# Down projections of the second pair of sequences as transposed seven-product quarters

## The chip, the cores and the metric

The kernel runs on one core of one Trainium2 chip. The metric is the device time of one execution in microseconds (us). The engines are TensorE (PE in the rows, its weight loads PEld), VectorE (DVE), ScalarE (ACT), GpSimd (POOL) and SyncE (SP, whose row SPq is the DMA queue that it issues on).

## The reference

For four sequences of 512 tokens with 512 features: a cross-attention weight is added to `x`, and then a routed feed-forward block. Cut to what the change touches:

```python
gate = einsum('btd,edf->ebtf', x, Wg); up = einsum('btd,edf->ebtf', x, Wu)   # 8 experts, D = F = 512
mid = silu(gate) * up
out = einsum('ebtf,efd->ebtd', mid, Wd)          # the down projection
y = x + einsum('bte,ebtd->btd', weights, out)    # router weights per token and expert
```

Two experts also have low-rank additions to Wg, Wu and Wd; the kernel merges these into the weights first. All is float32. The kernel splits each float32 operand into a high and a low part and makes three passes (high x high, low x high, high x low) for each product.

## The kernel before, in words

After attention and the first expert (up to about 205 us) come `STEPS` = 14 rounds of one expert each on a pair of sequences: rounds 0 to 6 on sequences 0 and 1, rounds 7 to 13 on sequences 2 and 3 (`SWAP` = 7 is the first of these). Two sequences and the halves of the 512 features give a 2 x 2 block problem, and so gate and up are computed by Strassen's method in Winograd's form: seven products where a plain one has eight. Each of gate and up is worked in two halves of output rows, so that a round k has four "quads": j = 4k (gate, first half), 4k+1 (gate, second half), 4k+2 (up, first half), 4k+3 (up, second half). `quad(j, pending)` (before L1630) issues products 1, 5, 6, 3, 2, 7, each of two feature tiles by three passes, six matmuls of 128x128 weights on 512 columns. Product 4 of quad j (`fourth`) is issued inside the next quad, after its product 5, since it waits for VectorE to have read the bank (`c_made[C22]`).

The sums around the products are VectorE's and ScalarE's. For each quad VectorE makes four sums of weight quarters (`piece_sums`, L1168), ScalarE rounds the seven weight operands to their high parts (`piece_high_part`, L818), VectorE subtracts for the low parts (`piece_low_part`, L1182), and only then may product 1 begin (`piece_ready`). Three piece buffers rotate; SyncE loads one when the quad that used it has finished its product 4 (`load_next_piece`, L372). From the products ScalarE copies P1, P5 and U2 out of PSUM (`copy_p1`, `copy_p5`, `copy_u2`, L828 to L844), VectorE combines (`combine`, L1206), ScalarE applies silu (`gate_silu`), VectorE multiplies gate by up (`make_mid`, L1219), and each of the eight mid tiles gets a high part (ScalarE) and a low part (`mid_low_part`, L1262).

The down projection of round k-1 is plain: `down_half` (L1673) for each sequence, 4 token tiles by 4 feature tiles by 3 passes, 96 matmuls for the two, in the middle of round k, on the four banks `tiles`. Its weights are one load of 1 MB with one high and one low part (`wd_high_part`, `wd_low_part`). VectorE adds the four results of each half into `xacc`, scaled by the token's router weight (`add_down`, L1235), since tokens are on the partitions.

Each engine runs a list written out by hand, in program order; a wait holds all that is behind it on the same engine. VectorE's list for a round is the loop at L1386.

Of the kernel before, what the change touches and what calls it, by code (L numbers as in the profile page):

```python
# [10 lines left out]
P = 128  # L11
# [46 lines left out]
GATE, UP = 0, 1  # L58
# [9 lines left out]
def xattn_ffn_kernel(nc, x, xT, ctxT, wkT, bk, gamma, beta, wg, wu, wd, loraT, lora, wr, temperature, out):  # L68
# [6 lines left out]
    with ExitStack() as ctx:  # L75
# [33 lines left out]

        lora_a, lora_b, lora_w = (at(name, kb, shape) for name, kb, shape in  # L110
# [31 lines left out]
        s1_sb = nc.alloc_sbuf_tensor_at("s1_sb", [P, S], fp32, offset=beta_at)  # L142
        x_spill = nc.dram_tensor("x_spill", [2, 2, P, KT * S], fp32, kind="Internal").ap()
        x21_spill = nc.dram_tensor("x21_spill", [P, 2 * S], fp32, kind="Internal").ap()
        acc_spill = nc.dram_tensor("acc_spill", [P, 2 * TT * D], fp32, kind="Internal").ap()
# [140 lines left out]
        piece_ready = [sem(f"piece_ready{i}") for i in range(3)]  # L286
        wd_loaded = sem("wd_loaded")
# [53 lines left out]

        def mids_before(j):
# [17 lines left out]
        def _(sp):  # L360
# [4 lines left out]
            def load_piece(j):  # L365
                k, m, f = j // 4, j % 4 // 2, j % 2
                source = weights_of(k, m).rearrange("(k p) f -> p k f", p=P)
                for g, cols in ((0, f + 2), (1, f)):
                    sp.dma_start(piece[j % 3][:, 2 * g:2 * g + 2, :].rearrange("p g (k c) -> p (g k) c", k=2),
                                 source[:, :, cols * P:(cols + 1) * P]).then_inc(piece_loaded[j % 3], 16)  # L370

            def load_next_piece(j):  # L372

                if j < 4 * STEPS:
                    sp.wait_ge(p_mm[4], j - 2)
                    load_piece(j)
# [109 lines left out]
            for k in range(1, STEPS):  # L486
# [23 lines left out]
                sp.wait_ge(d_mm, 8 * k)  # L510
                load_wd(k)
                if k == SWAP:
# [3 lines left out]
                    sp.dma_start(xacc[:, 2 * TT * D:], acc_spill).then_inc(acc_loaded, 16)  # L516
# [5 lines left out]
                if k < len(LORA_JOBS):  # L522
                    store_merged(k)
            for i in range(2 * TT):
                store_out(2 * TT + i, 8 * (STEPS - 1) + i + 1)
# [4 lines left out]
        def _(pool):  # L530
# [101 lines left out]
            pool.wait_ge(x_stored, 64)  # L632
            load_again(0, 0, 1)
            load_again(1, 2, 3)
            load_again(0, 2, 2)


        @block.scalar
        def _(act):
# [178 lines left out]
            def piece_high_part(j):  # L818
                if j < 4 * STEPS:
                    act.wait_ge(piece_summed[j % 3], 4 * (j // 3) + 4)  # L820
                    nc.scalar.activation(piece_hi[j % 3][:, :, :], piece[j % 3][:, 1:8, :], ACT.Copy)\  # L821
# [1018 lines left out]
```

## Time and profile before

| | |
|---|---|
| median of three runs | 1055.22 us (1054.95 to 1056.51) |
| the profiled execution | 1055.69 us, of which the span of the profile is 1054.0 us |
| PE busy | 1042.4 us, 99% |
| PE weight loads | 853.0 us, 81% |
| DVE busy | 708.8 us, 67% |
| ACT busy | 449.5 us, 43% |
| POOL busy | 50.4 us, 5% |

Busy time of an engine is time covered by at least one of its instructions. A single matmul of 512 columns is shown with 389 ns, yet matmuls overlap: what one costs in a stream is the distance of two starts. The same is to be seen on DVE, where an instruction can begin before the end of the one before it. The granted TensorE clock was full in every slice.

### The profile page before, as it was taken

To read this page: it belongs to the slowest core of one execution; us is meant where nothing else is said; L and a number is where in the kernel's file an instruction comes from. 1 tells how busy PE (TensorE), PEld (TensorE's weight loads), DVE (VectorE), ACT (ScalarE), POOL (GpSimd) and SP (SyncE) were. 2 spreads that over 40 slices of the span, in tenths; PEclk is the share of its full clock that TensorE was granted. 3 is DMA by queue.
4 is the path that set the end of the run, shared out by engine and by line. 5 is a ranking of instruction groups with operands and counts; after the bars stand their busy time and mean duration, and the time that the engine had idled before them with its cause. 6 is when DMAs were issued, how large, how long until landed. Compare 5 with 4: busy or idle time off the path is not lost.

```text
span 1054.0 us, 12230 instructions
## 1 busy us (share of the span) xinstructions
PE 1042.4 (99%) x4680; PEld 853.0 (81%) x4680; DVE 708.8 (67%) x1212; ACT 449.5 (43%) x653; POOL 50.4 (5%) x62
## 2 busy tenths in 40 slices
PE   8999999999999999999999999999999999999998
PEld 5887787878888888888888888788888888888887
DVE  7878678877484866838487684847566473838544
ACT  4654363554442543444344344525334343524430
POOL 2511121100000000000000000000000000000000
PEclk9999999999999999999999999999999999999999
DMA  9410104334151322415135537202021121112012
GB/s 297 156 50 1 81 21 160 106 94 140 60 148 32 125 75 81 140 61 145 35 115 165 177 103 239 59 23 80 23 78 41 60 60 60 41 40 79 21 41 80
DMA packets 91307, 94.73 MB, mean 90 GB/s; under 512 B 4464, under 2 KB 67056, under 8 KB 90352
## 3 DMA queue, kind: packets, MB, share of 16 engines
q1 hardware_dynamic: 90096, 90.73, 27.4%
q0 software_dynamic: 864, 3.15, 1.0%
q8 instruction: 37, 0.61, 0.2%
q14 instruction: 22, 0.18, 0.1%
q10 hardware_dynamic: 288, 0.07, 0.0%
HBM read 76.63 MB, written 17.30 MB: 89 GB/s over the span
## 4 chain that ended last, share of the span: by engine, by line
PE 86%; DVE 8%; issue 2%; ACT 2%; DMA 1%; POOL 0%; SPq 0%; DVEq 0%
PE gate_up L1621 15%; PE gate_up L1623 15%; PE gate_up L1622 15%; PE tiles L1508 10%; PE tiles L1510 10%; PE tiles L1509 10%; PE gate_up L1579 2%; PE gate_up L1580 2%; PE gate_up L1585 2%; PE tiles L1544 1%; DVE piece_lo L1187 1%; DMA wd_raw<-in_wd_dram 1%; DVE mids_lo L1265 1%; DVE xacc L1239 1%; DVE tx_lo L1248 0%
## 5 line engine op out<-in xcount | busy, mean ns | idle before, releaser
L1621 PE MATMUL gate_up<-xT_hi,piece_hi 128*128 128x512 f32 x448 | 174.8, 390 | 1.0 <-DVE mids L1226 0.6
L1508 PE MATMUL tiles<-wd_hi,mids_hi 128*128 128x512 f32 x448 | 174.4, 389 | 0.4 <-DVE mids_lo L1265 0.4
L1623 PE MATMUL gate_up<-xT_lo,piece_hi 128*128 128x512 f32 x448 | 174.4, 389 | 0.0
L1622 PE MATMUL gate_up<-xT_hi,piece_lo 128*128 128x512 f32 x448 | 174.4, 389 | 0.0
L1509 PE MATMUL tiles<-wd_lo,mids_hi 128*128 128x512 f32 x448 | 174.3, 389 | 0.0
L1510 PE MATMUL tiles<-wd_hi,mids_lo 128*128 128x512 f32 x448 | 174.3, 389 | 0.0
L1239 DVE SCALAR_TENSOR_TENSOR xacc<-tiles,rw,xacc 128x512 f32<-128x512 f32 x112 | 78.0, 750 | 138.5 <-PE tiles L1510 138.5
L1187 DVE TENSOR_TENSOR piece_lo<-piece,piece_hi 128x1024 fp32r<-128x1024 f32 x112 | 118.2, 1097 | 28.9 <-ACT piece_hi L821 27.6
L1621 PE MATMUL gate_up<-tx_hi,piece_hi 128*128 128x512 f32 x336 | 130.9, 389 | 0.3 <-DVE gates L1216 0.3
L1622 PE MATMUL gate_up<-tx_hi,piece_lo 128*128 128x512 f32 x336 | 130.8, 389 | 0.0
L1623 PE MATMUL gate_up<-tx_lo,piece_hi 128*128 128x512 f32 x336 | 130.8, 389 | 0.0
L834 ACT ACTIVATE gate_up<-gate_up 128x512 f32<-128x512 f32 x56 | 32.6, 582 | 208.7 <-PE gate_up L1623 201.2
L861 ACT ACTIVATE mids_hi<-mids 128x512 fp32r<-128x512 f32 x112 | 70.4, 629 | 85.5 <-DVE mids L1226 45.4
L821 ACT ACTIVATE piece_hi<-piece 128x1792 fp32r<-128x1792 f32 x56 | 95.2, 1700 | 24.0 <-DVE piece L1180 24.0
L1621 PEld LDWEIGHTS gate_up<-xT_hi,piece_hi 128*128 128x128 f32 x448 | 84.1, 188 | 20.9 <-issue 1.4
L1508 PEld LDWEIGHTS tiles<-wd_hi,mids_hi 128*128 128x128 f32 x448 | 84.1, 188 | 18.3 <-DVE mids_lo L1265 0.8
L1623 PEld LDWEIGHTS gate_up<-xT_lo,piece_hi 128*128 128x128 f32 x448 | 84.1, 188 | 17.5
L1510 PEld LDWEIGHTS tiles<-wd_hi,mids_lo 128*128 128x128 f32 x448 | 84.1, 188 | 17.4
L1509 PEld LDWEIGHTS tiles<-wd_lo,mids_hi 128*128 128x128 f32 x448 | 84.1, 188 | 17.4
L1622 PEld LDWEIGHTS gate_up<-xT_hi,piece_lo 128*128 128x128 f32 x448 | 84.1, 188 | 17.1
L1265 DVE TENSOR_TENSOR mids_lo<-mids,mids_hi 128x512 fp32r<-128x512 f32 x112 | 77.0, 688 | 6.9 <-ACT mids_hi L861 4.9
L1621 PEld LDWEIGHTS gate_up<-tx_hi,piece_hi 128*128 128x128 f32 x336 | 63.1, 188 | 13.9 <-DVE gates L1216 0.7
(176 smaller groups left out, 1406.2 us busy)
## 6 DMA issues: line engine op xcount, KB each, us to landing
piece<-in_wg_dram SPq DMA_DIRECT2D x40, 256.0 KB, 3.2
piece<-in_wu_dram SPq DMA_DIRECT2D x40, 256.0 KB, 3.3
wd_raw<-in_wd_dram SPq DMA_DIRECT2D x10, 1024.0 KB, 5.3
piece<-merged SPq DMA_DIRECT2D x32, 256.0 KB, 3.3
merged<-lora_w SPq DMA_DIRECT2D x6, 1024.0 KB, 4.3
x_back<-x_spill SPq DMA_DIRECT2D x9, 512.0 KB, 5.3
wd_raw<-merged SPq DMA_DIRECT2D x4, 1024.0 KB, 5.6
out_dram<-xacc SPq DMA_DIRECT2D x16, 256.0 KB, 4.1
```

Source lines behind the costliest of these rows:

```text
L821: nc.scalar.activation(piece_hi[j % 3][:, :, :], piece[j % 3][:, 1:8, :], ACT.Copy)\
L834: nc.scalar.activation(gate_up[:, BANK_C, :], gate_bank(j), ACT.Copy).then_inc(s1_made, 1)
L861: nc.scalar.activation(mids_hi[h][:, f, :], mids[h][:, f, :], ACT.Copy).then_inc(mids_hi_made, 1)
L1187: ins = nc.vector.tensor_tensor(piece_lo[j % 3][:, first:last, :], piece[j % 3][:, first:last, :], plain(piece_hi[j % 3][:, first - 1:last ...
L1239: nc.vector.scalar_tensor_tensor(tile_of(b, t), tiles[:, t, :], rw[:, (b * TT + t) * E + s:(b * TT + t) * E + s + 1], tile_of(b, t), ALU.m ...
L1265: nc.vector.tensor_tensor(mids_lo[h][:, f, :], mids[h][:, f, :], plain(mids_hi[h][:, f, :]), ALU.subtract)\
L1508: nc.tensor.matmul(dst, w_h, x_h, start=first, stop=False)
L1509: nc.tensor.matmul(dst, w_h, x_l, start=False, stop=False)
L1510: return nc.tensor.matmul(dst, w_l, x_h, start=False, stop=last)
L1621: nc.tensor.matmul(dst, w_h, x_h, start=first and kt == 0, stop=False, skip_group_check=True)
L1622: nc.tensor.matmul(dst, w_l, x_h, start=False, stop=False, skip_group_check=True)
L1623: ins = nc.tensor.matmul(dst, w_h, x_l, start=False, stop=last and kt == 1, skip_group_check=True)
```

## The change

For rounds 7 to 12 (the second pair, all but the last expert) the down projection is no longer plain. It is computed transposed (output features on the partitions, tokens along the free dimension) and by the same seven products, in two halves `down_quad(d)`, d = 2(k-7) and 2(k-7)+1. The last round's down projection (13) stays plain.

- Down weights are now quarters like gate's and up's: they are loaded as pieces, and get `piece_sums`, a high and a low part each. `QUADS` lists the order of all pieces; in rounds 8 and on it is gate 0, gate 1, down 0, down 1, up 0, up 1.
- The mid tiles need operand sums of their own: `mix_of` makes T1 to T4 for both feature tiles, and seven operands for each of the two have a high and a low part.
- With tokens along the free dimension the router weight can no longer be a scalar per partition. Gates are multiplied by a router row instead (`scale_gates`, two instructions of 1024 elements for each half), the rows being made by one transpose, a store and broadcast loads (`turn_rw`, `load_rw_rows`).
- The results are added into a transposed accumulator `acc_t` (`add_u2_and_p5`, `add_c12`, `add_c11`, `add_c22`, `add_c21`), with three copies by ScalarE for each half.
- In the last round `acc_t` is turned back by 32 TensorE transposes in two groups (`turn_back`) and added to `xacc` (`add_turned_back`), which is reloaded only in round 13 (before: round 7).

PE's order in rounds 8 to 13, and VectorE's list for such a round:

```diff
+            for k in range(SWAP + 1, STEPS):
+                j, d = 4 * k, 2 * (k - SWAP - 1)
+                quad(j, True)
+                quad(j + 1, True)
+                down_quad(d)
+                down_quad(d + 1)
+                quad(j + 2, False, d + 1)
+                if k == STEPS - 1:
+                    turn_back(0)
+                quad(j + 3, True)
             down_half(STEPS - 1, 0, 4 * STEPS - 1)
```

```diff
+            def operands_of_first(k):
+                combine(k, UP, 0, C12)
+                make_mid(k, 0, C12)
+                if k > SWAP:
+                    piece_low_part(NUMBER[k, UP, 1])
+                piece_low_part(NUMBER[k + 1, GATE, 0])
+                combine(k, UP, 0, C22)
+                make_mid(k, 0, C11)
+                make_mid(k, 0, C22)
+                mix_of(k, 0, T1)
+                operand_low_part(k, 0, B11)
+                mix_of(k, 0, T2)
+                mix_of(k, 0, T3)
+                operand_low_part(k, 0, T1)
+                operand_low_part(k, 0, B22)
+                make_mid(k, 0, C21)
+                mix_of(k, 0, T4)
+                combine(k, UP, 1, C12)
+                make_mid(k, 1, C12)
+                operand_low_part(k, 0, T2)
+                operand_low_part(k, 0, T3)
+                operand_low_part(k, 0, B21)
+                operand_low_part(k, 0, T4)
...
+            for k in range(SWAP + 1, STEPS):
+                j, d = 4 * k, 2 * (k - SWAP - 1)
+                last = k == STEPS - 1
+                combine(k - 1, UP, 1, C22)
+                make_mid(k - 1, 1, C11)
+                piece_sums(NUMBER[k, GATE, 1])
+                mix_of(k - 1, 1, T1)
+                operand_low_part(k - 1, 1, B11)
+                make_mid(k - 1, 1, C22)
+                piece_low_part(NUMBER[k, GATE, 1])
+                mix_of(k - 1, 1, T2)
+                mix_of(k - 1, 1, T3)
+                operand_low_part(k - 1, 1, T1)
+                operand_low_part(k - 1, 1, B22)
+                make_mid(k - 1, 1, C21)
+                mix_of(k - 1, 1, T4)
+                combine(k, GATE, 0, C12)
+                operand_low_part(k - 1, 1, T2)
+                operand_low_part(k - 1, 1, T3)
+                combine(k, GATE, 0, C22)
+                operand_low_part(k - 1, 1, B21)
+                operand_low_part(k - 1, 1, T4)
+                piece_sums(NUMBER[k - 1, DOWN, 0])
+                combine(k, GATE, 1, C12)
+                piece_low_part(NUMBER[k - 1, DOWN, 0])
+                combine(k, GATE, 1, C22)
+                if not last:
+                    scale_gates(k, 0)
+                piece_sums(NUMBER[k - 1, DOWN, 1])
+                add_u2_and_p5(d)
+                add_c12(d)
+                piece_low_part(NUMBER[k - 1, DOWN, 1])
+                add_c11(d)
+                add_c22(d)
+                piece_sums(NUMBER[k, UP, 0])
+                if not last:
+                    scale_gates(k, 1)
+                add_c21(d)
+                add_u2_and_p5(d + 1)
+                piece_low_part(NUMBER[k, UP, 0])
+                add_c12(d + 1)
+                add_c11(d + 1)
+                add_c22(d + 1)
+                piece_sums(NUMBER[k, UP, 1])
+                add_c21(d + 1)
+                if last:
+                    combine(k, UP, 0, C12)
+                    piece_low_part(NUMBER[k, UP, 1])
+                    make_mid(k, 0, C12)
+                    combine(k, UP, 0, C22)
+                    make_mid(k, 0, C11)
+                    mid_low_part(k, 0, C12)
+                    add_turned_back(0)
+                    make_mid(k, 0, C22)
...
+                    mid_low_part(k, 0, C21)
+                    wd_low_part(k)
+                    combine(k, UP, 1, C22)
+                    add_turned_back(1)
...
+                else:
+                    piece_sums(NUMBER[k + 1, GATE, 0])
+                    operands_of_first(k)
```

The load of a piece, ScalarE's order around a down quad, and what `down_quad` waits for:

```diff
+            def load_next_piece(n):
+                if n >= len(QUADS):
+                    return
+                k, which, m = QUADS[n - 3]
+                if which == DOWN:
+                    sp.wait_ge(q_mm, q_done(4, 2 * (k - SWAP) + m))
+                else:
+                    sp.wait_ge(p_mm[4], 4 * k + 2 * which + m + 1)
+                load_piece(n)
...
+                copy_q_u2(d)
+                piece_high_part(NUMBER[k - 1, DOWN, 1])
+                copy_q1(d + 1)
+                copy_q5(d + 1)
+                copy_q_u2(d + 1)
+                piece_high_part(NUMBER[k, UP, 0])
...
+            def down_quad(d):
+                n = NUMBER[SWAP + d // 2, DOWN, d % 2]
+                pe.wait_ge(piece_ready[n % 3], (n // 3 + 1))
...
+                down_product(d, 1, down_bank(d), first=True)
...
+                down_product(d, 5, tiles[:, BANK_B, :], first=True)
+                if d % 2 == 0:
+                    fourth(4 * (SWAP + 1 + d // 2) + 1)
+                else:
+                    down_fourth(d - 1)
...
+                down_product(d, 6, down_bank(d))
...
+                down_product(d, 3, tiles[:, BANK_B, :], last=True)
+                down_product(d, 2, tiles[:, BANK_C, :], last=True)
...
+                down_product(d, 7, down_bank(d))
```

## Rows read from the trace of the kernel before

**Rows 1.** The page's head and its section 1: share of the span.

```profile
span 1054.0 us, 12230 instructions
...
PE 1042.4 (99%) x4680; PEld 853.0 (81%) x4680; DVE 708.8 (67%) x1212; ACT 449.5 (43%) x653; POOL 50.4 (5%) x62
```

**Rows 2.** Windows: us, PE, PEld, DVE, ACT, POOL busy (x), PEclk, DMA share, GB/s.

```profile
757.90:817.80 59.90, 59.90 (x266) 49.58 (x265) 36.95 (x59) 24.30 (x33) 0.00 (x0) 1.00 0.18 53
```

**Rows 3.** PE's waits after 640 us: total, times, longest; two rows in all.

```profile
PE gate_up L1621 <- DVE mids L1226: 0.3, 1, 0.3
```

**Rows 4.** Timeline of PE: start, us, engine, line; first matmuls of four stretches.

```profile
648.25 0.39 PE L1621 MATMUL gate_up<-xT_hi,piece_hi 128*128 128x512 f32 x1
...
869.67 0.39 PE L1621 MATMUL gate_up<-xT_hi,piece_hi 128*128 128x512 f32 x1
...
871.03 0.39 PE L1621 MATMUL gate_up<-tx_hi,piece_hi 128*128 128x512 f32 x1
...
1027.43 0.39 PE L1508 MATMUL tiles<-wd_hi,mids_hi 128*128 128x512 f32 x1
```

**Rows 5.** Timeline of DVE in round 11: starts that follow one another without a wait.

```profile
888.24 2.79 DVE L1239 SCALAR_TENSOR_TENSOR xacc<-tiles,rw,xacc 128x512 f32<-128x512 f32 x4 [9.37 <-PE tiles L1510]
...
899.11 0.68 DVE L1229 TENSOR_TENSOR mids<-gates,gate_up 128x512 f32<-128x512 f32 x1
...
899.71 0.69 DVE L1265 TENSOR_TENSOR mids_lo<-mids,mids_hi 128x512 fp32r<-128x512 f32 x1
...
901.51 2.08 DVE L1187 TENSOR_TENSOR piece_lo<-piece,piece_hi 128x1024 fp32r<-128x1024 f32 x2
...
903.52 0.69 DVE L1265 TENSOR_TENSOR mids_lo<-mids,mids_hi 128x512 fp32r<-128x512 f32 x1
...
904.12 2.36 DVE L1195 TENSOR_TENSOR wd_lo<-wd_raw,wd_hi 128x1024 fp32r<-128x1024 f32 x2
...
906.39 0.68 DVE L1226 TENSOR_TENSOR mids<-gates,gate_up 128x512 f32<-128x512 f32 x1
...
913.72 0.42 DVE L1175 TENSOR_TENSOR piece<-piece 128x256 f32<-128x256 f32 x1
...
915.19 0.68 DVE L1212 TENSOR_TENSOR gates<-u_sb,gate_up 128x512 f32<-128x512 f32 x1
```

**Rows 6.** Timeline of DVE: an instruction that reads what the one before it wrote.

```profile
895.78 0.69 DVE L1212 TENSOR_TENSOR mids<-u_sb,gate_up 128x512 f32<-128x512 f32 x1 [3.30 <-PE gate_up L1623]
...
896.58 0.69 DVE L1233 TENSOR_TENSOR mids<-gates,mids 128x512 f32<-128x512 f32 x1
```

**Rows 7.** Timeline: from PE's products to ScalarE and VectorE.

```profile
873.75 0.39 PE L1621 MATMUL gate_up<-xT_hi,piece_hi 128*128 128x512 f32 x1
...
873.95 0.60 ACT L844 ACTIVATE u_sb<-gate_up 128x512 f32<-128x512 f32 x1 [0.76 <-PE gate_up L1623]
...
874.45 1.70 ACT L821 ACTIVATE piece_hi<-piece 128x1792 fp32r<-128x1792 f32 x1
...
875.38 0.69 DVE L1212 TENSOR_TENSOR gates<-u_sb,gate_up 128x512 f32<-128x512 f32 x1 [3.30 <-PE gate_up L1623]
...
876.18 2.09 DVE L1187 TENSOR_TENSOR piece_lo<-piece,piece_hi 128x1024 fp32r<-128x1024 f32 x2
```

**Rows 8.** From a finished product 4 to a load, and the loads' landing times.

```profile
631.93 0.39 PE L1508 MATMUL tiles<-wd_hi,mids_hi 128*128 128x512 f32 x1
...
632.12 0.92 SPq L369 DMA_DIRECT2D piece<-in_wu_dram  x2
...
DMA to landing us min/median/max: 2.8/3.2/5.9
...
xacc<-acc_spill SPq DMA_DIRECT2D x1, 2048.0 KB, 11.5
```

**Rows 9.** Timeline of PE: sixteen transposes and the matmul after them.

```profile
115.38 1.91 PE L1526 MATMUL gate_up<-w_raw 128*128 128x128 f32 x16
...
117.04 0.48 PE L1508 MATMUL tiles<-w_hi,mid_hi 128*128 128x512 f32 x1
```

More of the change, by code:

```diff
@@ L57 @@
 SWAP = POSITIONS - 1
-GATE, UP = 0, 1
+GATE, UP, DOWN = 0, 1, 2
+QUADS = [(k, which, m) for k in range(SWAP + 1) for which in (GATE, UP) for m in range(2)] \
+    + [(k - (which == DOWN), which, m) for k in range(SWAP + 1, STEPS) for which in (GATE, DOWN, UP) for m in range(2)]
+NUMBER = {quad: n for n, quad in enumerate(QUADS)}
+B11, T1, B22, T2, T3, B21, T4 = range(7)
+OPERAND = {1: B11, 5: T1, 6: T2, 3: B22, 2: B21, 7: T3, 4: T4}
 BANK_B, BANK_C = 1, 2
@@ L485, in _ @@
             store_merged(0)
-            for k in range(1, STEPS):
+            for k in range(1, SWAP + 1):
                 if k < len(LORA_JOBS):
@@ new lines, in operand_low_part, with add_to_turned @@
+            def operand_low_part(k, kt, o):
+                dve.wait_ge(operand_hi_made, 14 * (k - SWAP) + 7 * kt + o + 1)
+                raw, hi, lo = operand_of(o, kt)
+                nc.vector.tensor_tensor(lo, raw, plain(hi), ALU.subtract).then_inc(operand_ready, 1)
+            def add_to_turned(d, c, source):
+                m = d % 2
+                h, tile = 1 if c in (C12, C22) else 0, m if c in (C12, C11) else m + 2
+                to = acc_t[:, tile, h, :]
+                nc.vector.tensor_tensor(to, to, source, ALU.add).then_inc(q_added, 1)
@@ new lines, in add_c21, with add_turned_back @@
+            def add_c21(d):
+                dve.wait_ge(q_mm, q_done(4, d))
+                if d >= 2:
+                    dve.wait_ge(q_added, q_add("c21", d - 2))
+                add_to_turned(d, C21, down_bank(d))
+            def add_turned_back(h):
+                dve.wait_ge(acc_loaded, 16)
+                for t in range(TT):
+                    dve.wait_ge(back_mm, 4 * h + t + 1)
+                    nc.vector.tensor_tensor(tile_of(2 + h, t), tile_of(2 + h, t), tiles[:, t, :], ALU.add).then_inc(back_added, 1)
@@ L1417, in _ @@
                     combine(k, GATE, 1, C22)
-                    combine(k, UP, 0, C12)
+                    scale_gates(k, 0)
+                    scale_gates(k, 1)
+                    piece_sums(j + 4)
+                    operands_of_first(k)
+                    break
                 elif k > 0:
@@ L1628, in fourth, with down_product @@
                 product(j, 4, gate_bank(j), last=True)
-            def quad(j, pending):
+            def down_product(d, i, dst, first=False, last=False):
+                n = NUMBER[SWAP + d // 2, DOWN, d % 2]
+                hi, lo = piece_hi[n % 3], piece_lo[n % 3]
+                pe.wait_ge(operand_ready, 14 * (d // 2) + 7 + OPERAND[i] + 1)
+                for kt in range(2):
+                    cols = slice(kt * P, (kt + 1) * P)
+                    w_h, w_l = hi[:, COMBO[i] - 1, cols], lo[:, COMBO[i], cols]
+                    raw, x_h, x_l = operand_of(OPERAND[i], kt)
+                    nc.tensor.matmul(dst, w_h, x_h, start=first and kt == 0, stop=False, skip_group_check=True)
+                    nc.tensor.matmul(dst, w_l, x_h, start=False, stop=False, skip_group_check=True)
+                    ins = nc.tensor.matmul(dst, w_h, x_l, start=False, stop=last and kt == 1, skip_group_check=True)
+                ins.then_inc(q_mm, 1)
@@ L1779, in _ @@
             pe.wait_ge(mid_made, EARLIER + B * FT + UNIT_CREDIT)
-            for k in range(STEPS):
+            for k in range(SWAP + 1):
                 j = 4 * k
```

356 lines of the change are left out of this document (301 added, 55 removed).

## The prediction

> **What bounds the kernel now.** I read the page's section 1 first: PE is busy 99% of the span, DVE 67%, ACT 43% [rows 1]. Then the windows by round: a round of the second pair takes 59.9 us, PE covers all of it, DVE 36.95 us, ACT 24.3 us, and the granted clock is 1.00, the 2.4 GHz level [rows 2]. The waits confirm it: after 640 us PE waited for another engine twice, 0.5 us in all [rows 3]. So TensorE is the bound, and removed matmuls are removed time as long as the others keep up. What one costs is read from starts, not durations: two products of six matmuls start 1.36 us apart [rows 4], 226.7 ns for a matmul. A round has 4 quads of 42 matmuls and 96 for the down projection, 264 x 0.2267 = 59.85 us.
>
> The question is then whether DVE, with 23 us to spare in a round, keeps up with what the change gives it.
>
> **PE's gain.** A down projection goes from 96 matmuls to 2 x 42 = 84, in rounds 8 to 13: 72 x 0.2267 = 16.3 us less. PE's minimum for a round is 42 products x 1.36 = 57.1 us.
>
> **PE's addition.** 32 transposes: sixteen took 1.66 us before the next matmul started [rows 9], so 3.3 us, and one more in round 6 with its wait, some 0.2 us beside ScalarE's conversions. If all else hid, the sum would be 1055.2 - 16.3 + 3.5 = 1042.4 us.
>
> **DVE's load in a round.** Distances of starts [rows 5]: an instruction on 512 elements 0.60 us (899.11 to 899.71); the two of a piece's low part 2.01; two on 1024 elements 2.27; the four of `piece_sums` 1.47; one that reads what the instruction ahead of it wrote takes 0.20 more [rows 6]. The load before: 24 x 0.60 + 4 x 1.47 + 4 x 2.01 + 2.27 + 8 `add_down` (four cover 2.79) 5.4 + 0.4 = 36.4 us, against 36.95 measured [rows 2], so the count holds. After, in rounds 8 to 12: on 512 elements 8 `combine`, 8 `make_mid`, 8 `mix_of`, 14 `operand_low_part` and 12 adds, 50 x 0.60 = 30.0; `scale_gates` 4 x 1.14 = 4.5; six sums 8.8; six low parts 12.0; six close dependences 1.2. That is 56.6 us, against PE's 57.1. Mixes, scalings and adds are new, but have the form of instructions shown (both operands in SBUF, or one in PSUM). The nearest slower row, `add_down` at 0.68, would give 58.2; nothing in a row speaks for less than 0.60. I take 0.60.
> Here a rule can be weighed. In the trace an instruction lasts 0.69 us and the next starts after 0.60 [rows 5]. By the Trainium skill, "VectorE: DVE Perf Modes", section "The DRAIN you can't avoid", the next instruction does not start until the pipeline is empty. By that rule the 50 would cost 0.69 each, 4.5 us more a round; the trace disagrees for this kernel, so I don't count it.
>
> ACT gains 6 copies (0.50 us apart [rows 7]), 6 more operand roundings, two piece roundings of 1.7 for one of 1.9: about 8 us on 24.3. It is not a bound, but it stands in a chain below. At nothing I cost POOL's identity and its zeroing of `acc_t` (POOL is idle after the first fifth, and the first add comes in round 8), the router rows' loads (asked for half a round ahead; in round 7 they take the place of the 2 MB reload in SP's queue, behind the stores of the first pair and ahead of a piece that is held by its buffer anyway), and the 1 MB weight load of rounds 7 to 12, which goes. If the rows came late in round 7, `scale_gates` would hold S once, by a microsecond or two.
>
> **Whether DVE at 99% can keep pace.** Only without idling, and its list has waits on PE in it. I follow one round. Number PE's products: gate quads 0 to 6 and 7 to 13, down quads 14 to 20 and 21 to 27, up quads 28 to 34 and 35 to 41; the third place of each quad is the product 4 of the quad before. S is when DVE starts `combine(k, UP, 0, C12)`. It needs place 32 done, plus 0.27 us (product 3 starts at 873.75 and so ends at 875.11, DVE starts at 875.38 [rows 7]). F is when PE starts place 9 of the next round, product 4 of gate 0, which waits for `combine(k+1, GATE, 0, C22)`.
>
> S to F on DVE is one unbroken run: 34 instructions on 512 elements (19 in `operands_of_first`, 15 at the head of the next round) 20.4 us, three low parts 6.0, one `piece_sums` 1.47, four close dependences 0.8: 28.7 us. PE has 18 products there (33 to 41, 0 to 8), 24.5 us, and ends up waiting. From F, PE must do places 9 to 32, 24 x 1.36 = 32.6, and 0.27, before the next S. So a round can't be shorter than 28.7 + 32.6 + 0.3 = 61.6 us, though both engines have less than 57.2 us of work. That is already over 59.85.
>
> Three further waits lie on this loop.
> (a) The piece rounded for the next quad stands behind the copy of U2 in ScalarE's list (`copy_u2`, `copy_q_u2`). End of product 6 to copy 0.20, copy 0.50, rounding 1.73 to DVE's start (873.75, 873.95, 874.45, 876.18 in [rows 7]), low part 2.10, 0.05 to PE: 4.58 us. PE has three products left in the quad, 4.08 us. So 0.5 us before each of places 14, 21 and 28: 1.5 us. Behind the waiting DVE are the accumulations; they have room (8 us of work in 10).
> (b) `piece_sums` of the next round's gate 0 stands ahead of `operands_of_first`. Its buffer is freed by place 30. From there: 0.19 us to the first of two issues, 0.46 to the second, landing 3.2 [rows 8], 0.05, sums 1.47: S at 5.4 us after place 30, instead of 2.72 + 0.27 = 3.0. Costs 2.4 us. DVE idles, and all operands are queued behind it. Ends: 2.0 with the shortest landing of 2.8, 5.1 with the longest of 5.9; I take the median.
> (c) The low part of up 1 stands after S, so PE waits some 3.7 us at place 35. This is not on the loop: PE still reaches place 8 before DVE frees it.
> A round: 61.6 + 1.5 + 2.4 = 65.5 us. Bounds: 61.6 with neither, and 68 with 0.68 for the new forms in S to F, the slower landing in part, and 0.1 to 0.2 us for PE's restart after each of four waits, which no row shows cleanly.
>
> **The sum against the profiled execution.** Round 7's up 0 starts at 648.25 [rows 4]; nothing before it moves. Place 30 ends 4.08 later, at 652.33; S of round 7 by (b) at 657.7. The next round has no low part of up 1 in the run: S of round 8 at 657.7 + 63.5 = 721.2. Four rounds more: 721.2 + 4 x 65.5 = 983.2 for S of round 12. From there F, then places 9 to 30 with three waits of 0.5: 28.7 + 29.9 + 1.5 + 0.1 = 60.2, so place 30 of round 13 ends at 1043.4.
> The tail, in us from there. `acc_spill`, 2 MB, is asked for only now and took 11.5 to land [rows 8]; it is moved from round 7, where it delayed nobody, to round 13, where `add_turned_back(0)` stands ahead of `make_mid(k, 0, C22)` in DVE's list. So DVE waits until 12.1 and turns back until 14.5; `make_mid` C22 ends at 15.1. ScalarE rounds that mid ahead of `copy_p5`, and PE's place 39 waits for that copy until 16.3 (it would be there at 12.6). Then places 39 and 40, 16 transposes and 41: to 22.2. `combine` C22, then the first tile of `add_turned_back(1)`: the last `down_half` starts at 23.8, at 1067.2. In the kernel before it started at 1027.43 [rows 4] and the span ended 26.6 later. So 1067.2 + 26.6 = 1093.8, and 1.7 for what lies around the span (1055.69 - 1054.0): 1095.5 us. The profiled execution stands 0.5 us over the median. Forecast 1095 us, 3.8% slower.
>
> **The rivals.**
> 1. PE stays the bound and the gain comes. For it: DVE's sum of work is under PE's, and 23 us were free. Then only the tail costs: without its waits 1042.4, with the 5.5 us by which the reload holds the last `down_half` (23.8 against 15.0 + 3.3) 1047.9 us. It decides on the other side once a round is under 59.85 us. For that the loop S to F to S would have to be 1.8 us shorter than its instructions alone, and that needs starts under 0.55 us apart. 6%.
> 2. The loop is there, but (a) and (b) are smaller: rounds of 61.6 to 63.5 us. With neither, S of round 7 at 655.3, then 59.6 and 4 x 61.6, 58.7 to the end of place 30, 23.8 of tail and 28.3 to the end: 1072 us. With rounds of 63.5, about 1083. 17%.
> 3. PE's clock falls. It was 1.00 throughout [rows 2], but PE never stood still for 3.7 us there, as it would at place 35 and at the tail. By the Trainium skill, "TensorE: Matmul & The Clock Gate", section "HAM oscillation — how this bites in real kernels", idle gaps of this kind bring the array back to half clock. Its price from rows: a product at 1.2 GHz takes 2.7 us. A few are absorbed, since PE is ahead of DVE between S and F; were all of places 35 to 41 and the next 7 slow, PE would be late at place 8 by 6.5 us, and five rounds cost 33 us: 1127 us. 5%.
> 4. Within 0.2% of before: what DVE adds to a round and the 2.7 us that PE saves in it cancel. A coincidence, 2%.
> That the change doesn't do what it says would show as 1055 us and is in rival 4.
>
> **How the numbers follow.** The forecast, a round of 64 to 67 us and the end between 1085 and 1105, has 70%; it is the likeliest. The range goes down into rival 2 and up over slower restarts: 1073 to 1112 us. A change of under 0.2% can't be told from none in this measurement. Faster by more 6%, within 2%, slower 92%.
>
> **What would show each step.** Windows by round: about 65.5 us each from round 8 on, DVE busy 57, PE busy under 58. PE's waits: on DVE `gates` (`combine`) once or twice a round, on `piece_lo` four times, the one at up 1 the longest (3 to 4 us). DVE's waits: `piece` on the DMA some 2 to 3 us a round. Matmuls still 226.7 ns apart, clock 1.00. In the tail, a wait of some 4 us of `xacc` on the reload. I am wrong if DVE's starts are closer than 0.6 us, or if PE's waits on DVE total less than 3 us a round.

## The result, and the profile after

The changed kernel takes 1099.92 us, median of three runs (1099.79 to 1100.25), against 1055.22: a ratio of 1.0419 with a 95% interval of 1.0404 to 1.0435. The forecast was 1095 us, in a range of 1073 to 1112.

The page of the changed kernel, head and section 1, and the granted clock of section 2:

```profile
span 1098.2 us, 12671 instructions
...
PE 1050.6 (96%) x4641; PEld 844.5 (77%) x4641; DVE 832.0 (76%) x1412; ACT 497.9 (45%) x732; POOL 55.0 (5%) x65
...
PEclk9999999999999999999999999989999999998999
```

Against [rows 1], PE issues fewer matmuls and still takes longer; no engine is at its limit over the span. DVE does 123 us more.

Windows of the changed kernel (us, then PE, PEld, DVE, ACT and POOL busy, granted clock, DMA share, GB/s): one round from S to S, then two stretches of 4 us right after the longest wait of PE in that round.

```profile
922.24:988.69 66.45, 61.08 (x254) 47.90 (x252) 56.58 (x91) 32.48 (x46) 0.00 (x0) 0.97 0.19 56
926.00:930.00 4.00, 4.00 (x11) 3.12 (x11) 4.00 (x6) 0.96 (x2) 0.00 (x0) 0.57 0.02 4
930.00:934.00 4.00, 4.00 (x19) 3.28 (x18) 3.92 (x8) 3.51 (x8) 0.00 (x0) 1.00 0.19 58
```

Where [rows 2] had 59.90 us with PE busy in all of it, a round is 66.45 us; DVE is busy in 56.58 of them, and idle in the other 10.

PE's waits after 640 us (total, times, longest), which were two rows in [rows 3], 0.5 us together:

```profile
PE gate_up L1987 <- DVE piece_lo L1374: 18.5, 11, 3.5
PE gate_up L1987 <- ACT p_sb L931: 5.9, 7, 1.3
PE tiles L2005 <- DVE piece_lo L1374: 4.0, 12, 0.3
PE gate_up L1987 <- DVE mids L1403: 3.3, 3, 1.7
PE gate_up L1987 <- DVE mids L1415: 2.2, 6, 0.4
PE tiles L1873 <- DVE xacc L1540: 1.5, 1, 1.5
```

DVE's waits from 720 to 1045 us in the same kernel:

```profile
DVE acc_t L1499 <- ACT down_u L980: 10.3, 10, 2.0
DVE gates L1399 <- PE gate_up L1989: 9.5, 5, 1.9
DVE piece L1364 <- DMA piece<-in_wg_dram: 9.0, 3, 3.1
DVE acc_t L1499 <- PE tiles L2007: 6.8, 5, 1.8
DVE piece L1364 <- DMA piece<-merged: 5.9, 2, 3.0
```

The two engines take turns: each waits for the other, and the loads of the next gate piece hold DVE five times for 3 us.

The loop's own timeline in round 11 of the changed kernel (start, us, engine, line, what; in brackets the idle time and its releaser). First from the load to S, then PE's places 35, 9, 14, 21 and 28:

```profile
917.25 0.69 DVE L1499 TENSOR_TENSOR acc_t<-acc_t,tiles 128x512 f32<-128x512 f32 x1 [1.25 <-PE tiles L2007]
...
920.77 0.43 DVE L1364 TENSOR_TENSOR piece<-piece 128x256 f32<-128x256 f32 x1 [2.83 <-DMA piece<-merged]
...
922.24 0.68 DVE L1399 TENSOR_TENSOR mids<-u_sb,gate_up 128x512 f32<-128x512 f32 x1
...
925.80 0.50 PE L1987 MATMUL gate_up<-xT_hi,piece_hi 128*128 128x512 f32 x1 [3.15 <-DVE piece_lo L1374]
...
926.46 0.63 PE L1989 MATMUL gate_up<-xT_lo,piece_hi 128*128 128x512 f32 x1
...
926.89 0.63 PE L1987 MATMUL gate_up<-xT_hi,piece_hi 128*128 128x512 f32 x1
...
950.53 0.68 DVE L1403 TENSOR_TENSOR gates<-p_sb,gate_up 128x512 f32<-128x512 f32 x1
...
951.27 0.50 PE L1987 MATMUL gate_up<-tx_hi,piece_hi 128*128 128x512 f32 x1
...
958.69 0.50 PE L2005 MATMUL tiles<-mids_hi,piece_hi 128*128 128x512 f32 x1 [0.33 <-DVE piece_lo L1374]
...
968.86 0.50 PE L2005 MATMUL tiles<-mids_hi,piece_hi 128*128 128x512 f32 x1 [0.33 <-DVE piece_lo L1374]
...
979.05 0.50 PE L1987 MATMUL gate_up<-xT_hi,piece_hi 128*128 128x512 f32 x1 [0.33 <-DVE piece_lo L1374]
```

S is at 922.24, F at 951.27, the next S at 988.69. Every piece of the forecast's loop is there: the unbroken run to `combine(k+1, GATE, 0, C22)` at 950.53, F behind it, the small waits before 14, 21 and 28, the load ahead of S.

Measured by S, as starts in the timelines (us), the kernels of this study stand so. "Seven" is round 7; "six rounds" runs to S of round 13, and "a round" is their mean; "tail" runs from there to the span's end. In the changed kernel the first of the six has no low part of up 1 between S and F, and nothing waits for a load at the end of the last; rounds 8 to 11 are 67.3, 66.4, 66.2 and 66.5.

| kernel | S of seven | six rounds | a round | tail | span |
|---|---|---|---|---|---|
| before | 655.3 | 360.1 | 60.0 | 38.5 | 1054.0 |
| after | 657.5 | 396.2 | 66.0 | 44.4 | 1098.2 |
| e1_sums_later | 655.0 | 393.6 | 65.6 | 44.6 | 1093.2 |
| e2_short_scaling | 657.7 | 394.3 | 65.7 | 44.4 | 1096.4 |
| e3_short_mid | 657.9 | 389.7 | 64.9 | 44.6 | 1092.1 |
| e5_round_first | 657.8 | 383.7 | 63.9 | 44.2 | 1085.7 |
| e6_lows_later | 658.1 | 389.6 | 64.9 | 44.5 | 1092.3 |
| e8_rebalanced | 655.1 | 375.1 | 62.5 | 43.7 | 1073.9 |
| e9_bank_free | 654.9 | 347.0 | 57.8 | 43.8 | 1045.6 |

The 44.2 us that the span grew are 2.2 before S of round 7, 36.1 in six rounds, 5.9 in the tail.

### The profile page after: what moved, and what is told of

Same layout as the page of the kernel before. It is cut to its first block, busy times and chain, and to the rows that moved or that the text cites. A ratio compares the mean times of both kernels' runs of the same rounds, so it can differ in the third digit from the quotient of the medians.

```text
span 1098.2 us, 12671 instructions
## 1 busy us (share of the span) xinstructions
PE 1050.6 (96%) x4641; PEld 844.5 (77%) x4641; DVE 832.0 (76%) x1412; ACT 497.9 (45%) x732; POOL 55.0 (5%) x65
## 3 DMA queue, kind: packets, MB, share of 16 engines
q0 software_dynamic: 864, 3.15, 0.9%
## 4 chain that ended last, share of the span: by engine, by line
PE 63%; DVE 19%; issue 6%; ACT 6%; DMA 3%; SPq 0%; DVEq 0%; POOL 0%; ACTq 0%
PE gate_up L1987 10%; PE gate_up L1989 10%; PE gate_up L1988 10%; PE tiles L1873 6%; PE tiles L1875 6%; PE tiles L1874 6%; DVE piece_lo L1374 4%; ACT piece_hi L913 3%; PE tiles L2005 2%; PE gate_up L1944 2%; PE gate_up L1945 2%; PE gate_up L1950 2%; PE tiles L2007 2%; PE tiles L2006 2%; DVE mids_lo L1492 2%
## 5 line engine op out<-in xcount | busy, mean ns | idle before, releaser
L1374 DVE TENSOR_TENSOR piece_lo<-piece,piece_hi 128x1024 fp32r<-128x1024 f32 (+1 forms) x136 | 142.9, 1096 | 23.0 <-ACT piece_hi L913 20.9
L926 ACT ACTIVATE gate_up<-gate_up 128x512 f32<-128x512 f32 x56 | 32.6, 582 | 187.3 <-PE gate_up L1989 126.8
L1873 PE MATMUL tiles<-wd_hi,mids_hi 128*128 128x512 f32 x256 | 99.8, 390 | 2.0 <-DVE xacc L1540 1.5
L1875 PE MATMUL tiles<-wd_hi,mids_lo 128*128 128x512 f32 x256 | 99.6, 389 | 0.0
L1874 PE MATMUL tiles<-wd_lo,mids_hi 128*128 128x512 f32 x256 | 99.6, 389 | 0.0
L1430 DVE SCALAR_TENSOR_TENSOR xacc<-tiles,rw,xacc 128x512 f32<-128x512 f32 x64 | 44.5, 750 | 70.9 <-PE tiles L1875 70.9
L1988 PEld LDWEIGHTS gate_up<-tx_hi,piece_lo 128*128 128x128 f32 x336 | 64.4, 192 | 13.4
L1989 PEld LDWEIGHTS gate_up<-tx_lo,piece_hi 128*128 128x128 f32 x336 | 63.9, 190 | 13.9
L953 ACT ACTIVATE mids_hi<-mids 128x512 fp32r<-128x512 f32 x64 | 40.2, 629 | 58.6 <-DVE mids L1415 27.1
L1873 PEld LDWEIGHTS tiles<-wd_hi,mids_hi 128*128 128x128 f32 x256 | 48.1, 188 | 12.7 <-issue 1.9
L1944 PE MATMUL gate_up<-xT_hi,w_hi 128*128 128x512 f32 (+1 forms) x160 | 55.1, 360 | 1.6 <-POOL w_lo L664 0.8
```

The source lines that it names most:

```text
L926: nc.scalar.activation(gate_up[:, BANK_C, :], gate_bank(j), ACT.Copy).then_inc(s1_made, 1)
L953: nc.scalar.activation(mids_hi[h][:, f, :], mids[h][:, f, :], ACT.Copy).then_inc(mids_hi_made, 1)
L1374: ins = nc.vector.tensor_tensor(piece_lo[j % 3][:, first:last, :], piece[j % 3][:, first:last, :], plain(piece_hi[j % 3][:, first - 1:last ...
L1430: nc.vector.scalar_tensor_tensor(tile_of(b, t), tiles[:, t, :], rw[:, (b * TT + t) * E + s:(b * TT + t) * E + s + 1], tile_of(b, t), ALU.m ...
L1873: nc.tensor.matmul(dst, w_h, x_h, start=first, stop=False)
L1874: nc.tensor.matmul(dst, w_h, x_l, start=False, stop=False)
```

## The experiments

The theory: a loop S, DVE's unbroken run, F, PE's 24 products, S sets the round, made by the order of DVE's and ScalarE's lists. The rivals: DVE's total work (57 us of a round, 99% of PE's least of 57.1) sets it; or the fallen clock does. Each time below is the median of four executions.

**The sums out of S's way.** e1 takes wait (b) away: the sums of the next gate piece go behind the low part of up 1.

```diff
@@ operands_of_first
-                piece_low_part(NUMBER[k + 1, GATE, 0])
+                piece_sums(NUMBER[k + 1, GATE, 0])
                 combine(k, UP, 0, C22)
                 make_mid(k, 0, C11)
+                piece_low_part(NUMBER[k + 1, GATE, 0])
@@ list, end of a round (likewise in round 7)
-                    piece_sums(NUMBER[k + 1, GATE, 0])
                     operands_of_first(k)
```

> One edit to the changed kernel: the four weight sums of the next round's gate 0, which wait for a load that is asked for when product 4 of the second down quad is done, stand 2.9 to 3.6 us later in VectorE's list, after the low part of up 1. Loop theory (a round is VectorE's unbroken run from S to F plus PE's places 9 to 32): the wait on the load, 2.8 to 3.1 us a round, goes, but the sums (1.47 us) now lie inside the run, so S comes 2.3 us earlier and F only 0.9 us; six loops give -5 us. TensorE's wait at up 1 falls from 3.2 to 3.5 us to under 1 us, so the clock should stay at the 2.4 GHz level, -1 to -2 us more: 1092 to 1095 us. Rival (the wait on the load is lost time as such): all of 2.9 us a round comes back, six times: 1082 us.

1095.12 us (1094.6 to 1095.57), ratio 1.0377 [1.0361, 1.0392]. DVE's waits from 720 to 1040 us have no `piece` on a DMA any more; this one is new:

```profile
DVE mids L1399 <- PE gate_up L1988: 8.4, 4, 2.1
```

S now waits for PE's place 32, 2.3 us earlier, as the loop says; but the sums (1.47) and a wait of 0.57 for ScalarE's rounding of the moved piece are now in the run, which grows from 28.2 to 30.2 us. In round 10 the clock was 1.00 in both kernels, so the two can be compared there: S to `combine` C22 takes 28.19 and 30.19, the rest of the round 37.98 and 35.73, the whole 66.17 and 65.92. The load costs 2.3 us where it stands, yet to move it behind S returns 0.25 of them.

Over the six rounds the table shows 0.4 a round (66.04 to 65.61), and the clock has its part in it. It stayed at 1.00 in e1, where PE's wait at place 35 is 0.96. In the changed kernel S to `combine` C22 takes 29.3 us in rounds 8 and 12, with a mean granted clock of 0.95, and 28.2 or 28.3 in rounds 9 to 11, with 0.97 to 1.00: 1.1 us in two of six rounds, 0.4 a round on the mean. In the last round, where nothing had waited for the load, the moved sums cost more than that: it is 0.8 longer. e1 also saves 2.6 us up to S of round 7, where no rounded piece of up 1 lies in the run. This was not in the expectation; without it the time would be some 1097.7, where 1092 to 1095 stood. The rival, that the whole wait comes back (1082), falls, and so does the clock as what sets the round: at 1.00 throughout, a round of e1 is still 65.9 us.

**DVE's total, off the loop.** e2 takes 4.0 us a round from DVE, between F and S.

```diff
@@ scale_gates
-                    two = gates[m][:, 2 * pair:2 * pair + 2, :]
-                    nc.vector.tensor_tensor(two, two, rw_rows[:, :, :], ...)
+                    two = gates[m][:, 2 * pair:2 * pair + 2, 0:32]
+                    nc.vector.tensor_tensor(two, two, rw_rows[:, :, 0:32], ...)
```

> Leaves out part of the computation: the router scaling of the gates covers 32 of 512 tokens, in all four instructions of a round, so VectorE's load falls by 4 x 1.0 = 4.0 us a round. They stand between F and the next S, where VectorE also waits for TensorE. Loop theory: no change at all, 1099.9 us within 1 us. Rival (VectorE's total load, 57 us a round, sets the time): -4 us a round, six times, 1076 us.

1098.6 us (1098.12 to 1099.09), ratio 1.041 [1.0394, 1.0425]. DVE's busy time fell by 23 us, the time by 1.3. The rival of the total, 1076, falls. Of the 1.3 us most is the clock's: one round (from 854.41) with a granted clock of 0.95 and 29.5 us from S to `combine` C22, where the changed kernel has two such rounds.

```profile
PE 1049.4 (96%) x4641; PEld 843.8 (77%) x4641; DVE 808.6 (74%) x1412; ACT 497.7 (45%) x732; POOL 55.1 (5%) x65
```

**DVE's run, on the loop.** e3 takes 2 us a round from DVE, between S and F.

```diff
@@ make_mid
+                n = slice(0, 32) if SWAP <= k < STEPS - 1 else slice(0, S)
-                    nc.vector.tensor_tensor(target, gates[m][:, c, :], target, ...)
+                    nc.vector.tensor_tensor(target[:, n], gates[m][:, c, n], target[:, n], ...)
```

> Leaves out part of the computation: of the eight gate times up multiplications of a round (rounds 7 to 12), the four on C12 and C22 cover 32 of 512 tokens, 0.5 us less each, 2.0 us a round, half of what the shortened scaling saves. All four stand in VectorE's run from S to F. Loop theory: -2.0 us a round, six loops, -12 us, and 1 us more where TensorE's wait at up 1 gets too short for the clock to fall: 1086 to 1088 us. Rival (total load): the same -12 us here, but twice that for the shortened scaling. Rival (TensorE or the loads set the round): no change.

1093.86 us (1092.06 to 1094.24), ratio 1.0361 [1.0346, 1.0377]: 6 us less, where the expectation had 12. The timeline of DVE from S at 919.29 shows why:

```profile
926.75 0.69 DVE L1493 TENSOR_TENSOR mids_lo<-mids,mids_hi 128x512 fp32r<-128x512 f32 x1 [0.52 <-ACT mids_hi L962]
...
939.05 2.09 DVE L1374 TENSOR_TENSOR piece_lo<-piece,piece_hi 128x1024 fp32r<-128x1024 f32 x2 [0.47 <-ACT piece_hi L913]
```

The shorter run meets ScalarE, which had been just ahead of it, and waits 1.0 of the 2.0 us. S to `combine` C22 fell from 28.3 to 27.3, and the six rounds together by 6.5. Half the DVE time of e2, taken from this place, gives nearly five times the gain (6.1 against 1.3 us): the place counts. The run's next limit lay only 1 us below it.

**The rounding ahead of the copy.** e5 takes wait (a) away.

```diff
@@ ScalarE's list; likewise before copy_q_u2(d) and copy_q_u2(d + 1)
-                copy_u2(j + 1)
                 piece_high_part(NUMBER[k - 1, DOWN, 0])
+                copy_u2(j + 1)
@@ DVE's list: each low part ahead of the step that reads the copy
-                combine(k, GATE, 1, C12)
                 piece_low_part(NUMBER[k - 1, DOWN, 0])
+                combine(k, GATE, 1, C12)
```

> The changed kernel with one edit in the stretch F to S: ScalarE rounds the next piece ahead of its U2 copy, and VectorE takes that piece's low part ahead of the additions that wait for the U2 copy (down 0, down 1, up 0). The run from S to F is as it was. Loop theory: TensorE no longer waits before places 14, 21 and 28, 0.67, 0.65 and 0.67 us a round as measured with the restarts (7.42, 10.17 and 10.19 us against 6.80 and 9.52), so -2.0 us a round, six times: 1086 to 1089 us. Rival (VectorE's total load sets the round): the same work, no change, 1100 us.

1087.04 us (1086.12 to 1088.85), ratio 1.0297 [1.0282, 1.0312]. The waits at places 14, 21 and 28 are gone and a round is 2.1 us shorter: the three starts of 0.33 us were worth 0.7 each, since after such a wait the next two matmuls start 0.71 and 0.34 us behind the ones before them, where 0.23 is the rule. That is 0.6 each of lost time.

**The low parts behind F.** e6 moves six low parts of the down operands (of T2, T3, B21, T4; 3.6 us) out of the run, to the places where the down products first need them.

```diff
@@ list
                 combine(k, GATE, 0, C12)
-                operand_low_part(k - 1, 1, T2)
-                operand_low_part(k - 1, 1, T3)
                 combine(k, GATE, 0, C22)
...
+                for o in (T2, B21):
+                    for kt in range(2):
+                        operand_low_part(k - 1, kt, o)
@@ down_product: the wait by a table in the new order
-                pe.wait_ge(operand_ready, 14 * (d // 2) + 7 + OPERAND[i] + 1)
+                pe.wait_ge(operand_ready, 14 * (d // 2) + READY[OPERAND[i]])
```

> The changed kernel with one edit: the low parts of T2, T3, B21 and T4 of both feature tiles are taken after F instead of before it. VectorE's work is the same, its run from S to F is shorter by six low parts, 3.6 us: 25.4 us, as long as TensorE's 18 products and its wait at up 1. After F they lengthen the stretch from down 0 to down 1 by 0.5 to 1 us, where VectorE had less than that free. Loop theory: -2.5 to -3 us a round, six times, and TensorE's wait at up 1 stays, so the clock still falls in some rounds: 1082 to 1086 us. Rival (total load): no change, 1100 us.

1092.59 us (1091.72 to 1094.08), ratio 1.0345 [1.0327, 1.0362]: 7 us less, not 14 to 18. Two lines of its timeline from S at 918.41:

```profile
921.97 0.74 PE L1987 MATMUL gate_up<-xT_hi,piece_hi 128*128 128x512 f32 x1 [3.28 <-DVE piece_lo L1375]
...
933.48 0.69 DVE L1404 TENSOR_TENSOR mids<-p_sb,gate_up 128x512 f32<-128x512 f32 x1 [1.21 <-PE gate_up L1989]
```

DVE's run shrinks by 2.35 us only, as DVE now waits for PE, and `combine` C22 starts 25.9 after S. PE itself reaches place 9 no earlier than 27.7 after S: it started place 35 3.6 us behind S, ran part of up 1 at the lower clock, and stands once more before place 7:

```profile
943.26 0.47 PE L1987 MATMUL gate_up<-xT_hi,piece_hi 128*128 128x512 f32 x1 [0.35 <-DVE mids L1416]
```

L1416 is `make_mid` C21 of up 1, which reads the bank that place 7 writes. So under the loop through `combine` C22 lies a second one, through place 35, PE, DVE and that bank, about 1.3 us shorter. And the down quads wait 0.92 for 0.33 at place 21, behind the added low parts. To win all of it, the low part of up 1 has to come ahead of S too, and the bank has to come free earlier.

**All of it together.** e8 takes the edits of e1, e5 and e6, puts the low part of up 1 before S, where DVE has time, spreads ScalarE's roundings of the operands, takes both `combine` of gate 0 between the mixes, changes the order of the additions into `acc_t`, and in the tail puts `wd_low_part` ahead of `add_turned_back(0)`. All instructions are the same, in another order.

```diff
@@ operands_of_first
                 make_mid(k, 0, C12)
-                if k > SWAP:
-                    piece_low_part(NUMBER[k, UP, 1])
@@ list, ahead of operands_of_first
                 add_c21(d + 1)
+                piece_low_part(NUMBER[k, UP, 1])
@@ list, head of a round
+                combine(k, GATE, 0, C12)
                 mix_of(k - 1, 1, T2)
                 mix_of(k - 1, 1, T3)
+                combine(k, GATE, 0, C22)
```

> The whole computation of the changed kernel, with VectorE's and ScalarE's lists in another order: the low parts of T2, T3, B21 and T4 of both feature tiles (8 x 0.60 us) come after F, six of them out of the run; the low part of up 1 comes before S; the sums of the next gate 0 after S; ScalarE rounds the next piece before it copies U2; combinations of gate 0 come earlier. VectorE still has 56.6 us a round. Loop theory: the run from S to F is 24 to 25 us, as long as TensorE's 18 products there, so TensorE's 57.1 us plus about 1 us of restarts sets the round: 58 to 59 us, and with 3.3 us of transposes and some 2 us in the last round 1046 to 1056 us. Rival (total load): VectorE is as loaded as before, the round stays above 64 us, the time above 1085 us.

1076.85 us (1075.71 to 1079.03), ratio 1.021 [1.0193, 1.0228], 21 us over the top of what was expected. PE's waits after 640 us are two rows:

```profile
PE gate_up L1985 <- DVE mids L1417: 18.9, 6, 3.2
PE tiles L1871 <- DVE xacc L1542: 1.5, 1, 1.5
```

The timeline of PE gives the place, once a round:

```profile
804.69 0.77 PE L1985 MATMUL gate_up<-xT_hi,piece_hi 128*128 128x512 f32 x1 [3.13 <-DVE mids L1417]
```

It is place 7: the first product of gate 1 writes the PSUM bank from which `make_mid(k-1, 1, C21)` reads. The changed kernel has this wait too, the 0.4 on L1415, hidden there because PE is 0.2 us early at place 9 even after it; with the rest of the loop gone it is the loop. The edit had put two `combine` ahead of that `make_mid`. It still starts 23.9 us after S (803.86), 25.2 in the changed kernel, but PE now comes to place 7 some 4 us sooner (21.4 after S, 25.5 there).

PE's wait is now on the loop, and so is what the lower clock behind it costs. Windows of rounds 8, 9 and 10, S to S:

```profile
716.18:779.93 63.75, 60.45 (x254) 48.93 (x253) 56.24 (x91) 31.64 (x46) 0.00 (x0) 0.95 0.21 58
779.93:842.57 62.64, 59.37 (x254) 48.21 (x253) 56.24 (x91) 31.70 (x46) 0.00 (x0) 0.97 0.24 59
842.57:903.67 61.10, 57.79 (x254) 46.99 (x253) 56.26 (x91) 31.70 (x46) 0.00 (x0) 1.00 0.24 61
```

**That bank freed earlier.** e9 is e8 with one line moved.

```diff
                 make_mid(k - 1, 1, C22)
+                make_mid(k - 1, 1, C21)
                 piece_low_part(NUMBER[k, GATE, 1])
...
                 operand_low_part(k - 1, 1, B22)
-                make_mid(k - 1, 1, C21)
```

> The rebalanced kernel e8, whose trace showed a new wait of 3.1 to 3.2 us in every round: the first product of gate 1 writes the bank that the multiplication C21 of the second up half still reads, and I had put that multiplication 4 us later. Here it stands ahead of the low part of gate 1. Whole computation. Loop theory: the wait goes, with it the fall of the clock, rounds of 58.5 to 59.5 us instead of 61.1 to 63.7: 1051 to 1058 us. If VectorE's total load (56.6 us and what it must wait for) is the limit by now, rounds stay at 61 us: 1066 us.

**1047.67 us** (1047.05 to 1048.49), ratio to the kernel before 0.9922 [0.9908, 0.9937]: 0.8% faster than the kernel before. The head and section 1 of its page:

```profile
span 1045.6 us, 12671 instructions
...
PE 1031.8 (99%) x4641; PEld 840.3 (80%) x4641; DVE 827.8 (79%) x1412; ACT 493.7 (47%) x732; POOL 55.1 (5%) x65
```

Its window of a round, S to S, with the columns of [rows 2]:

```profile
886.21:944.04 57.83, 57.69 (x254) 47.00 (x253) 55.89 (x91) 31.62 (x46) 0.00 (x0) 1.00 0.23 64
```

The same 12671 instructions as in the changed kernel, 828 us of DVE for 832, and 52 us less. DVE is busy in 55.9 of 57.8 us and PE waits for nobody but once in the tail, 1.5 us. `combine` C22 starts 22.6 us after S (886.21 to 908.80); from there to F it is 0.7 as before, so the loop is 22.6 + 0.7 + 32.6 + 0.3 = 56.2 us, under PE's 57.1. Of the 28.1 us between the six rounds of e8 and those of e9 some 8.5 are the clock's (375.1 less 6 x 61.1), the rest is the wait.

**Is it DVE's total now?** e10 is e9 with the edit of e2.

> Leaves out part of the computation: e9 with the router scaling of the gates on 32 of 512 tokens, 4.0 us less VectorE work a round; the same edit that was made to the changed kernel as e2. Rounds of e9 take 57.8 us, TensorE's 42 products 57.1 us, VectorE is busy 56.1 us. If TensorE sets e9's round, only the few tenths in which it restarts behind VectorE can go: 57.2 to 57.8 us a round, 1044 to 1048 us. If VectorE's total load sets it, the round would fall further only if it were not held by TensorE, so nothing under 57.1 us: the test is whether the missing 0.7 us is VectorE's.

1047.35 us (1046.99 to 1047.99), ratio 0.9925 [0.9908, 0.9942]. With 4 us a round less on DVE the time is that of e9: the total doesn't set it. The 0.7 us by which e9's round stands over 57.1 come from elsewhere; starts of matmuls in that round show most of it:

```profile
917.22 0.50 PE L2003 MATMUL tiles<-mids_hi,piece_hi 128*128 128x512 f32 x1
917.55 0.40 PE L2004 MATMUL tiles<-mids_hi,piece_lo 128*128 128x512 f32 x1
...
929.39 0.39 PE L2005 MATMUL tiles<-mix_lo,piece_hi 128*128 128x512 f32 x1
...
929.91 0.47 PE L2003 MATMUL tiles<-mix_hi,piece_hi 128*128 128x512 f32 x1
...
930.22 0.40 PE L2004 MATMUL tiles<-mix_hi,piece_lo 128*128 128x512 f32 x1
```

Distances of 0.33, 0.52 and 0.31 for 0.23 make 0.5 with the 0.05 ahead of 917.22: place 14 just behind its piece's low part, and a product of T4 just behind T4's low part (DVE ends it at 929.77). That last cause is read from the times, not tested.

## Why the prediction was right, and where it was off

**The bound.** Right: 226.7 ns a matmul again, and in e9 a round of 57.8 us for PE's least of 57.1. The gain that the change holds is real: e9 has 2.0 of the 2.7 us a round, and gives 5.2 us back in the tail.

**DVE's load.** Right: 56.6 us counted, 56.58 busy in the window (56.5 to 56.7 in rounds 8 to 10). The forms that the trace of before didn't show start 0.60 us apart as assumed (mixes at 930.80 and 931.41). ScalarE was put at 24.3 + 8 = 32.3 us; it is 32.5. The forecast quotes a rule against its 0.60 us and finds that the trace disagrees. The same section of the Trainium skill, "VectorE: DVE Perf Modes", "The DRAIN you can't avoid", adds that a next instruction which is not held starts earlier, and with that the 0.60 us between starts agree.

**The loop.** Right in kind, and in size to 0.9 us in the round shown. Its pieces, forecast and measured: S to F 28.7 and 29.03; F to place 14 7.3 and 7.42; to 21 10.02 and 10.17; to 28 10.02 and 10.19; to S 9.48 and 9.64; the sum 65.5 and 66.45. The term that was mis-sized is PE's restart: the forecast held 0.1 to 0.2 for each of four waits back as a bound of its range, but put nothing into its sum. It makes 0.6 of the 0.9. The three waits themselves cost what was counted (starts 0.71 apart for 0.23, so 0.48 for 0.5), but behind F and behind each of them the second matmul starts 0.34 us after the first for 0.23, and the next ones lose a few hundredths more. The other 0.3 is S to F: 0.14 of it from `combine` C22 to F (0.74, counted as 0.60), the rest DVE's starts, more of which than the four counted stand over 0.60 apart.

From S of round 7 to place 30 of round 13 (at 1050.8) this makes 393.2 us, where 385.7 stood: 7.5 us. Some 2.2 of them are the clock's (Rival 3), the rest this 0.9 a round.

**Wait (b)** was put at 5.4 us from place 30 to S and was 5.2 at the first S shown and 5.4 at the second; S of round 7 at 657.7 was 657.54. e1 shows what the forecast had not asked: this wait can't be had back by moving the sums alone.

**Rival 3, the clock.** The fall that the forecast gave 5% did happen, and the forecast's own words, "clock 1.00", were wrong. After PE had stood for 3.15 us before place 35 the granted clock in the window from 926 was 0.57, that is mostly the 1.2 GHz level, with matmuls 0.43 us apart (926.46 to 926.89), and 1.00 again in the window from 930. The Trainium skill, "TensorE: Matmul & The Clock Gate", section "HAM oscillation — how this bites in real kernels", warns of just such waits, and the trace agrees after four of the five waits at place 35 (after 3.37 us at 859.63 the clock stayed at 1.00). But its price was not the 6.5 us a round of the rival. That figure doesn't follow from its own condition: 14 slow products take 19.0 us more, PE is ahead by 28.7 - 3.7 - 16 x 1.36 = some 3 us, and so it would be 16 us late; 6.5 is what seven slow products make.

In the round shown 11 matmuls started in 4 us for 17.6, some 1.5 us lost, and place 9 didn't suffer: PE still stood 0.81 us before place 4, 0.36 before place 7 and 0.2 before place 9. So "a few are absorbed" was right. Where more ran slow the loop did grow, by a way that the forecast hadn't named: the products of up 1 come late, and DVE's unbroken run has to wait for them. A line of round 8:

```profile
735.83 0.69 DVE L1399 TENSOR_TENSOR mids<-u_sb,gate_up 128x512 f32<-128x512 f32 x1 [0.56 <-PE gate_up L1989]
```

The windows of rounds 8 and 10, S to S:

```profile
722.40:789.70 67.30, 61.66 (x252) 48.67 (x252) 56.68 (x92) 32.24 (x46) 0.00 (x0) 0.95 0.21 55
856.07:922.24 66.17, 59.36 (x252) 46.68 (x252) 56.49 (x91) 32.28 (x46) 0.00 (x0) 1.00 0.22 56
```

Rounds 8 and 12 pay 1.1 us each, the others 0.3 or less: on the mean 0.4 us a round. In e8, where PE had nothing to spare at that place, the same fall costs 1.5 us at a clock of 0.97 and 2.7 at 0.95.

**The tail.** The reload's term was too large. In the view of the changed kernel's DMA transfers (count, KB each, us to landing) one line answers to the last of [rows 8]:

```profile
xacc<-acc_spill SPq DMA_DIRECT2D x1, 2048.0 KB, 8.5
```

And in its timeline:

```profile
1059.54 2.48 DVE L1540 TENSOR_TENSOR xacc<-xacc,tiles 128x512 f32<-128x512 f32 x4 [0.48 <-DMA xacc<-acc_spill]
...
1071.50 0.47 PE L1873 MATMUL tiles<-wd_hi,mids_hi 128*128 128x512 f32 x1 [1.54 <-DVE xacc L1540]
```

2 MB took 8.5 us for 11.5, so DVE waited 0.5 and not 4, and the last `down_half` starts 20.7 us after place 30, not 23.8. From there to the end 26.7, as forecast (26.6). That it landed faster because the DMA engines had less else to do there was not tested. So 1093.8 + 7.54 - 0.16 - 3.08 + 0.06 = 1098.16, the span. Here two errors of opposite sign met, 7.5 us too little in the rounds and 3.1 too much in the tail, and so the forecast of 1095 came nearer to 1099.92 than its rounds did.

**Rival 1**, that PE stays the bound, was rightly put low for this order of the lists, but for a reason that the forecast overstated: it argued that the loop would have to be shorter "than its instructions alone". The 28.7 us are the instructions of that order; e9 has 5.7 us less of them between S and `combine` C22, with no instruction less in the kernel. **Rival 2**, rounds of 61.6 to 63.5 us, is e8's region (61.1 to 63.9), where (a) and (b) are removed and more is moved; with (a) alone removed, in e5, full rounds are 64.2 to 65.6.

**What the later expectations missed** has one pattern. e3, e6 and e8 each shortened the binding loop rightly and priced what lay under it too low: ScalarE 1 us below; the loop through place 35 and the bank of `make_mid` C21 1.3 us below, of which e6's expectation named the wait at up 1 and counted on 2.5 to 3 us a round for 1.1 measured; that bank alone in e8, though its wait of 0.4 us stood in the traces already. Only e9, with no such loop left over 57.1, gave more than was asked (1047.7 for 1051 to 1058).

## What to carry to other kernels

Two engines with in-order lists that need each other make a loop, and its length, not either engine's share of busy time, is the round: follow one round from a hand-over, along one engine's list to where it releases the other, and back. To shorten it, move out of the stretch whatever the hand-over doesn't need, and before you run it look for the next loop within a few us of the one you cut: the banks and buffers that the first product of each group writes. An edit that adds 20 us of work a round to an engine with 23 us to spare wants its list ordered anew as a whole; here the order alone was worth 52 us in 1100.

## What the runs showed of the hardware that was not expected

- After waits of PE of 3.45, 3.14, 3.15 and 3.37 us (place 35 at 725.97, 793.26, 925.80 and 992.25) the granted clock was between 0.50 and 0.59 over the next 4 us; after 3.37 us at 859.63 it stayed at 1.00, as after the 0.96 us of e1. In e3 a wait of 2.67 us (place 35 at 725.00) was followed by 0.60. The length of the wait alone doesn't tell; what else counts stays open. The windows of the changed kernel behind 725.97 and behind 859.63:

```profile
726.00:730.00 4.00, 4.00 (x10) 3.13 (x11) 4.00 (x6) 0.79 (x2) 0.00 (x0) 0.50 0.01 4
...
860.00:864.00 4.00, 4.00 (x19) 3.31 (x18) 3.98 (x6) 1.13 (x3) 0.00 (x0) 1.00 0.02 4
```

- What a fall of the clock costs is set by what PE has to spare just there: a round with a mean granted clock of 0.95 is 1.1 us longer in the changed kernel and 2.7 in e8.
- A wait named as 0.33 us costs PE 0.6: the first matmul starts 0.71 and the next 0.34 after the one before, for 0.23.
- The same 2 MB reload landed in 11.5 us in the kernel before, at another point of the program, and in 8.5 in the one after (8.4 to 8.7 in the experiments).
